# The experts' router: two parts of its weight side by side, and eight short steps instead of four

## The chip, the core and the metric

The kernel runs on one core of a Trainium2 chip. The metric is device time in microseconds (us), one launch for the whole model, median over executions. The engines are named as in the profile: PE (TensorE's matmuls), PEld (its weight loads, which can overlap matmuls), DVE (VectorE), ACT (ScalarE), POOL (GpSimd), SP (the queue that issues the DMAs).

## What is computed

Two blocks of a perceiver on 2048 tokens of 256 features, in float32. The last sub-layer is a mixture of eight experts, and the router belongs to it:

```
xt = x.reshape(2048, 256)                       # normalised rows
logits = xt @ Wr + br                           # Wr: 256 x 8
gates = entmax_bisect(logits)                   # 25 bisection steps, alpha 1.5
gates = where(gates > 1e-9, gates, 0)
h = relu(einsum('td,edf->etf', xt, W1) + b1)    # 8 experts, 256 -> 1024
y = einsum('etf,efd->etd', h, W2) + b2          # 1024 -> 256
out = einsum('etd,te->td', y, gates)
```

The gates are needed only when the experts' outputs are summed.

## The kernel before

The rows are 16 tiles (`NT`) of 128 tokens, in four chunks (`NCH`) of 512. To keep float32 accuracy on the fast matmul path each operand is kept as a high part and a low part (what rounding to fp32r left over), and a product is made of three passes, high by high, high by low, low by high (`product3`, L78 to L85). Each pass runs over two blocks `kd` of 128 features (`KD`). So a product of one tile is six matmuls.

The decoder's last stage runs on TensorE as 256 steps, 32 for each expert: `hidden(e, n)` makes 128 hidden features of one chunk (six matmuls of 128x512), and `output(e, n - 1)` multiplies the hidden features of the step before by the second weight (twelve matmuls of 128x256). The order on TensorE is written out by hand (L1158 to L1170): in step n come `hidden(n)`, `output(n - 1)`, perhaps a side step of the recurrent cell or of the transposes of the experts' input (`in_step`, L830), and perhaps a router step. Side step "ro" is the cell's output projection (L1075), "mt" turns the normalised rows of two tiles (L1063), after which ACT copies the high part (L1222) and DVE makes the low part (L1453). The side steps "ro" of chunk 3 stand in steps 16 and 17, those of "mt" of chunk 3 in steps 21 and 22.

While TensorE goes on, ACT reads each hidden block twice with ReLU, once rounded and once not (`relu`, L1246 and L1247), and POOL subtracts (`low_half`, L935) to get the low part for the third pass of `output`. DVE, after its part of the side steps, splits expert 1's weights (`split_weights`, L1473 and L1476) and then waits for the router's last result and runs the bisection (`entmax`, L1581 to L1615), with sixteen pieces of the splitting of expert 2's weights in between (`split_piece`, L1485 and L1488). Expert 2's first `hidden` waits for the last of these pieces. The gated sums (L1624) begin after that.

`router(c)` does one chunk: for each of its four tiles six matmuls, in which the tile of `xt` (128 features by 128 tokens) is loaded as the weight and eight columns of `wrs` (the router's weight, 8 columns a part) are the moving operand. All matmuls of `product3` show line L83 in the profile; the router's are those with `dec_wrs`. The results lie in `router_bank`, 8 columns for each tile. It is called in steps 17, 18, 19 and 26.

Of the kernel before, what the change touches and what calls it, by code (L numbers as in the profile page):

```python
# [12 lines left out]
F32 = mybir.dt.float32  # L13
F32R = mybir.dt.float32r
I32 = mybir.dt.int32
ALU = mybir.AluOpType
# [3 lines left out]
P = 128  # L20
D = 256
KD = D // P
# [4 lines left out]
NT = T // P  # L27
# [50 lines left out]
def product3(pe, out, lhs, rhs, first=True, last=True):  # L78

    mm = None  # L80
    for k in range(KD):
        for n, (a, b) in enumerate(PASSES):
            mm = pe.matmul(out, lhs(a, k), rhs(b, k), start=first and k == 0 and n == 0,  # L83
                           stop=last and k == KD - 1 and n == 2)
    return mm  # L85
# [624 lines left out]
def decoder(nc, k, x_sb, banks, w, out):  # L710
# [7 lines left out]
    E, F = 8, 1024  # L718
# [5 lines left out]
    with ExitStack() as ctx:  # L724
        tools = Tools(nc, ctx, "dec")
# [7 lines left out]
        xt = tools.sb("xt", [P, NCH, 2, KD, CH], F32R)  # L733
# [12 lines left out]
        gate_bias, o_bias = tools.sb("gate_bias", [P, 4]), tools.sb("o_bias", [P, 1])  # L746
        z, o, f = (tools.sb(n, [P, SEG]) for n in ("z", "o", "f"))
        b1r, b1 = tools.sb("b1r", [E * NF, P]), tools.sb("b1", [P, E * NF])
        wr, wrs = tools.sb("wr", [P, KD, E]), tools.sb("wrs", [P, 2, KD, E], F32R)
        br = tools.sb("br", [P, E])  # L750

        part = lambda n: room[:, n * KD * CH:(n + 1) * KD * CH]
# [8 lines left out]
        with ExitStack() as inner:  # L761
# [13 lines left out]
            p = att.sb("p", [P, KD, R, S2])  # L775
# [14 lines left out]
        xs, dif, sq = (moe.sb(n, [P, NT, E]) for n in ("xs", "dif", "sq"))  # L790
# [16 lines left out]
        o_psum, o_rec, o_read, w_psum, x_att = sem("o_psum"), sem("o_rec"), sem("o_read"), sem("w_psum"), sem("x_att")  # L807
        x_bo = sem("x_bo")
        late_loads, side_psum, b_cols, wr_split = sem("late_loads"), sem("side_psum"), sem("b_cols"), sem("wr_split")
# [6 lines left out]
        e_high, router_psum, gates_ready, b2_in = sem("e_high"), sem("router_psum"), sem("gates_ready"), sem("b2_in")  # L816
# [3 lines left out]
        h_bank, y_bank, router_bank = banks[2:4], banks[4:8], banks[0]  # L820
# [142 lines left out]
        def _(pe):  # L963

            def turn_rows(c):
                for i in range(4):
                    t = 4 * c + i
                    pe.wait_ge(a_xn, t + 1)
                    if t >= 4:
                        pe.wait_ge(a_xt, t - 3)  # L970
                    for kd in range(KD):
                        mm = pe.transpose(banks[4 + i][:, kd * P:(kd + 1) * P], xn_a(t)[:, kd * P:(kd + 1) * P], k.ident[:, :])
                    mm.then_inc(a_psum, 1)
# [11 lines left out]
            def keys_proj(b):  # L985
                i, half = b // 2, b % 2
                if i >= 1:
                    pe.wait_ge(c_lo, i)
                if b >= 1:
                    pe.wait_ge(v_done, b)  # L990
                for m in range(KD):
                    mm = product3(pe, proj_bank[:, m * S2:(m + 1) * S2], lambda a, kd: wk[:, a, kd, m * P:(m + 1) * P],
                                  lambda a, kd: ctx_t[:, i % 2, a, kd, half * S2:(half + 1) * S2])
                mm.then_inc(k_psum, 1)
# [113 lines left out]
                if at == NF - 1:  # L1108
                    mm.then_inc(y_psum, 1)

            def router(c):
                pe.wait_ge(wr_split, 2)
                if c == 0:
                    pe.wait_ge(x_att, NT)
                for t in range(4 * c, 4 * c + 4):
                    mm = product3(pe, router_bank[:, t * E:(t + 1) * E], lambda a, kd: xt[:, c, a, kd, t % 4 * P:(t % 4 + 1) * P],
                                  lambda a, kd: wrs[:, a, kd, :])
                mm.then_inc(router_psum, 1)

            keys_proj(0)  # L1120
            turn_rows(0)
            turn_rows(1)
# [35 lines left out]
            for n in range(1, E * STEPS):  # L1158
                e = n // STEPS
                hidden(e, n % STEPS)  # L1160
                if n == 1:
                    project_output(NT - 1)
                output((n - 1) // STEPS, (n - 1) % STEPS)
                if n - 1 in in_step:
                    if n == 1:
                        pe.wait_ge(o_read, B)
                    side_step(*in_step[n - 1])
                if n in (17, 18, 19, 26):
                    router((17, 18, 19, 26).index(n))
            output(E - 1, STEPS - 1)  # L1170

        @block.scalar
        def _(act):
# [92 lines left out]
            queries(3)  # L1266
            act.wait_ge(side_psum, 1)
            act.copy(b1[:, :], banks[7][:, 0:E * NF]).then_inc(b_cols, 1)
            act.copy(wrs[:, 0], wr[:, :, :]).then_inc(wr_split, 1)
            for b in range(B):  # L1270
                if b == 4:
                    act.wait_ge(r_const, 4)
# [19 lines left out]
            for n in range(E * STEPS):  # L1292
                e = n // STEPS
# [13 lines left out]
        def _(dve):  # L1307
# [241 lines left out]
            def late_constants():  # L1549
                dve.wait_ge(late_loads, 16 * 20)  # L1550
                dve.tensor_scalar(wp[:, :], wp[:, :], 0.5, None, ALU.mult).then_inc(r_const, 1)
                dve.tensor_scalar(o_bias[:, :], gate_bias[:, 3:4], 0.5, None, ALU.mult).then_inc(r_const, 1)
                dve.wait_ge(wr_split, 1)
                dve.tensor_tensor(wrs[:, 1], wr[:, :, :], wrs[:, 0].bitcast(F32), ALU.subtract).then_inc(wr_split, 1)

            for b in range(B):
                slot_head(b)
# [19 lines left out]
            def go(ins):  # L1577
                s.give(ins)
                dve.wait_ge(s.sem, s.n)

            def entmax():  # L1581
                dve.wait_ge(router_psum, NCH)
                go(dve.tensor_tensor(xs[:, :, :], router_bank[:, 0:NT * E].rearrange("p (t e) -> p t e", e=E),
                                     br[:, :].unsqueeze(1).to_broadcast([P, NT, E]), ALU.add))
                go(dve.tensor_scalar(xs[:, :, :], xs[:, :, :], 0.5, None, ALU.mult))
                go(dve.tensor_reduce(top[:, :], xs[:, :, :], AX.X, ALU.max))
                s.give(dve.tensor_scalar(tau[:, :], top[:, :], 1.0, None, ALU.subtract))
                go(dve.tensor_scalar(dm[:, :], top[:, :], (1.0 / E) ** 0.5, None, ALU.subtract))
                go(dve.tensor_tensor(dm[:, :], dm[:, :], tau[:, :], ALU.subtract))
                go(dve.tensor_tensor(dif[:, :, :], xs[:, :, :], each(tau), ALU.subtract))  # L1590
                go(dve.scalar_tensor_tensor(out=sq[:, :, :], in0=dif[:, :, :], scalar=0.0, in1=dif[:, :, :],
                                            op0=ALU.max, op1=ALU.mult))
                go(dve.tensor_reduce(f_lo[:, :], sq[:, :, :], AX.X, ALU.add))
                go(dve.tensor_scalar(f_lo[:, :], f_lo[:, :], 1.0, None, ALU.subtract))
                for it in range(BISECTIONS):
                    step = 0.5 ** (it + 1)
                    if 8 <= it < 24:
                        split_piece(2, it - 8)
                    go(dve.scalar_tensor_tensor(out=tau_m[:, :], in0=dm[:, :], scalar=step, in1=tau[:, :],
                                                op0=ALU.mult, op1=ALU.add))  # L1600
                    go(dve.tensor_tensor(dif[:, :, :], xs[:, :, :], each(tau_m), ALU.subtract))
                    go(dve.scalar_tensor_tensor(out=sq[:, :, :], in0=dif[:, :, :], scalar=0.0, in1=dif[:, :, :],
                                                op0=ALU.max, op1=ALU.mult))
                    go(dve.tensor_reduce(f_m[:, :], sq[:, :, :], AX.X, ALU.add))
                    go(dve.scalar_tensor_tensor(out=f_m[:, :], in0=f_m[:, :], scalar=1.0, in1=f_lo[:, :],
                                                op0=ALU.subtract, op1=ALU.mult))
                    go(dve.scalar_tensor_tensor(out=inc[:, :], in0=f_m[:, :], scalar=0.0, in1=dm[:, :],
                                                op0=ALU.is_ge, op1=ALU.mult))
                    go(dve.scalar_tensor_tensor(out=tau[:, :], in0=inc[:, :], scalar=step, in1=tau[:, :],
                                                op0=ALU.mult, op1=ALU.add))  # L1610
                go(dve.tensor_reduce(f_m[:, :], sq[:, :, :], AX.X, ALU.add))
                go(dve.reciprocal(f_m[:, :], f_m[:, :]))
                go(dve.tensor_tensor(dif[:, :, :], sq[:, :, :], each(f_m), ALU.mult))
                dve.scalar_tensor_tensor(out=xs[:, :, :], in0=dif[:, :, :], scalar=THRESH, in1=dif[:, :, :],
                                         op0=ALU.is_gt, op1=ALU.mult).then_inc(gates_ready, 1)  # L1615
# [815 lines left out]
class Shared:  # L2431
# [5 lines left out]
    def sem(self, name):  # L2437
        return self.ctx.enter_context(self.nc.semaphore(name))
# [63 lines left out]
```

## Time and profile before

| | |
|---|---|
| median of 3 runs | 2103.95 us (2100.94 to 2104.42) |
| the profiled execution's own time | 2104.26 us |
| its span, first to last instruction | 2102.5 us |
| mean granted TensorE clock | 0.986 |
| PE busy | 2043.6 us, 97% |
| PEld busy | 1833.7 us, 87% |
| DVE, ACT, POOL busy | 1206.0, 1123.9, 498.2 us |

The busy time of an engine is summed over the whole program. The granted clock is the share of full speed (2.4 GHz) that the chip gave TensorE; 0.50 is 1.2 GHz. The times of instructions further down count from the span's start.

### The profile page before, as it was taken

Reading aid. Unit: us, or ns where it says so; the run is one execution under the profiler, and the core shown is the slowest. Engines: PE = TensorE matmul, PEld = TensorE weight load, DVE = VectorE, ACT = ScalarE, POOL = GpSimd, SP = SyncE. Lnnn points to the kernel's source line nnn. Section 1 sums busy time; section 2 is a strip of 40 time slices with the busy share of each in tenths; the row PEclk is TensorE's granted clock in tenths of the full one; section 3 lists DMA queues with packets and bytes.
Section 4 is the critical chain, followed back from the end, with each engine's and each line's share of the span. In section 5 each row is a group of like instructions: output and inputs, shape, how many; then the busy total and the mean of one; then the engine's idle time right before and its main releaser. Section 6 shows DMA issues by size and latency. Waiting matters only on the chain. (4 is left out here: it accounts for less than half of the span.)

```text
span 2102.5 us, 46360 instructions
## 1 busy us (share of the span) xinstructions
PE 2043.6 (97%) x18833; PEld 1833.7 (87%) x18833; DVE 1206.0 (57%) x3625; ACT 1123.9 (53%) x2556; POOL 498.2 (24%) x411
## 2 busy tenths in 40 slices
PE   7999999999999999799899999999999999999998
PEld 7999999999999999477768888789999999999998
DVE  6756565656565654567568898734937733242311
ACT  5556555656565655333258777643544444444443
POOL 1000020000000000123311222144444444444444
PEclk9999999999999999799999999999999999999999
DMA  4000200000000000100031110100110101101000
GB/s 151 22 17 22 77 22 17 22 16 22 17 24 28 17 7 2 45 1 1 1 94 36 32 32 22 42 1 1 61 41 1 41 1 41 41 1 41 1 11 31
DMA packets 48786, 57.81 MB, mean 27 GB/s; under 512 B 6528, under 2 KB 40128, under 8 KB 48448
## 3 DMA queue, kind: packets, MB, share of 16 engines
q1 hardware_dynamic: 48576, 54.85, 8.1%
q8 instruction: 151, 2.47, 0.5%
q14 instruction: 59, 0.48, 0.1%
HBM read 46.72 MB, written 2.10 MB: 23 GB/s over the span
## 5 line engine op out<-in xcount | busy, mean ns | idle before, releaser
L935 POOL TENSOR_TENSOR right_h<-right_hr,right_h 128x512 fp32r<-128x512 f32 x256 | 341.3, 1333 | 428.5 <-ACT right_hr L1247 428.5
L1246 ACT ACTIVATE right_h<-bank,dec_b 128x512 fp32r<-128x512 f32 x256 | 176.2, 688 | 399.5 <-PE bank L83 368.5
L83 PE MATMUL bank<-lat_wv,lat_kv_t 128*128 128x256 f32 (+1 forms) x1728 | 258.9, 300 | 0.7 <-issue 0.7
L83 PE MATMUL bank<-lat_kv_t,lat_qk 128*128 128x320 f32 x1536 | 254.7, 315 | 0.0
L83 PEld LDWEIGHTS bank<-lat_kv_t,lat_qk 128*128 128x128 f32 x1536 | 226.3, 188 | 7.7
L2208 ACT ACTIVATE lat_p<-bank,lat_neg_max 128x320 f32<-128x320 f32 x256 | 136.3, 532 | 173.8 <-DVE lat_neg_max L2332 173.8
L83 PEld LDWEIGHTS bank<-lat_wv,lat_kv_t 128*128 128x128 f32 x1728 | 222.9, 190 | 6.8 <-issue 1.1
L83 PE MATMUL bank<-dec_xt,dec_lo 128*128 128x512 f32 x512 | 202.1, 395 | 0.0
L1247 ACT ACTIVATE right_hr<-bank,dec_b 128x512 f32<-128x512 f32 x256 | 174.5, 682 | 0.0
L1727 POOL TENSOR_TENSOR lat_rs_rstdc<-lat_rs_varc,lat_rs_halfc 128x4 f32<-128x4 f32 x16 | 16.2, 1015 | 635.9 <-DVE lat_rs_varc L1719 635.9
L83 PE MATMUL bank<-dec_xt,dec_hi 128*128 128x512 f32 x512 | 164.2, 402 | 0.0
L1104 PE MATMUL bank<-dec_hi,right_h 128*128 128x256 f32 x1024 | 162.6, 280 | 0.5 <-POOL right_h L935 0.5
L1104 PE MATMUL bank<-moe_hi,right_h 128*128 128x256 f32 x1024 | 161.9, 280 | 0.7 <-POOL right_h L935 0.7
L1104 PE MATMUL bank<-dec_lo,right_h 128*128 128x256 f32 x1024 | 162.4, 281 | 0.0
L83 PE MATMUL bank<-dec_xt,moe_hi 128*128 128x512 f32 x512 | 159.8, 393 | 0.0
L1104 PEld LDWEIGHTS bank<-dec_hi,right_h 128*128 128x128 f32 x1024 | 148.3, 189 | 11.2 <-POOL right_h L935 0.9
L1104 PEld LDWEIGHTS bank<-moe_hi,right_h 128*128 128x128 f32 x1024 | 147.1, 188 | 11.9 <-POOL right_h L935 0.9
L2332 DVE TENSOR_REDUCE lat_neg_max<-bank 128x1 f32<-128x320 f32 x256 | 116.9, 484 | 46.9 <-PE bank L83 46.9
L1200 ACT ACTIVATE att_p<-att_sc,att_low 128x256 f32<-128x256 f32 x256 | 113.2, 511 | 53.0 <-DVE att_low L1355 53.0
L1104 PEld LDWEIGHTS bank<-dec_lo,right_h 128*128 128x128 f32 x1024 | 138.5, 188 | 0.0
L2327 DVE TENSOR_TENSOR lat_qk<-bank,lat_qk 128x256 fp32r<-128x256 f32 x256 | 90.8, 417 | 65.6 <-ACT lat_qk L2201 65.4
L1624 DVE SCALAR_TENSOR_TENSOR x_sb<-bank,moe_xs,x_sb 128x256 f32<-128x256 f32 x96 | 41.3, 473 | 144.9 <-PE bank L1104 144.9
(322 smaller groups left out, 3920.6 us busy)
## 6 DMA issues: line engine op xcount, KB each, us to landing
raw_w<-in_L_ffn_W SPq DMA_DIRECT2D x16, 1024.0 KB, 6.5
lat_ctx_raw<-in_ctx SPq DMA_DIRECT2D x16, 512.0 KB, 4.1
right_ctx_raw<-in_ctx_turned SPq DMA_DIRECT2D x16, 512.0 KB, 3.7
lat_kv_t<-lat_lt SPq DMA_DIRECT2D x32, 128.0 KB, 2.1
out_x<-x_sb SPq DMA_DIRECT2D x4, 512.0 KB, 2.9
x_sb<-in_x SPq DMA_DIRECT2D x1, 1792.0 KB, 14.5
lat_xl_now<-lat_xl SPq DMA_DIRECT2D x7, 256.0 KB, 4.8
ahead_room<-in_L_xattn_Wq SPq DMA_DIRECT2D x1, 1024.0 KB, 7.0
```

Source lines behind the costliest of these rows:

```text
L83: mm = pe.matmul(out, lhs(a, k), rhs(b, k), start=first and k == 0 and n == 0, stop=last and k == KD - 1 and n == 2)
L935: pool.tensor_tensor(h[:, g % 2, 1, :], hr[:, g % 2, :], h[:, g % 2, 0, :].bitcast(F32), ALU.subtract).then_inc(h_lo, 1)
L1104: mm = pe.matmul(y_bank[c % 2 * 2 + i // 2][:, i % 2 * D:(i % 2 + 1) * D], h[:, n % 2, b, i * P:(i + 1) * P], w2(e % 2, a)[:, at, :], star ...
L1200: act.activation(p[:, m, r, :], sc[:, m, r, :], ACT.Exp, bias=low[:, m, r:r + 1], scale=-1.0).then_inc(p_ready, 1)
L1246: act.activation(h[:, n % 2, 0, :], h_bank[n % 2][:, :], ACT.Relu, bias=bias).then_inc(h_hi, 1)
L1247: act.activation(hr[:, n % 2, :], h_bank[n % 2][:, :], ACT.Relu, bias=bias).then_inc(h_f, 1)
L1624: dve.scalar_tensor_tensor(out=x_sb[:, t, :], in0=src(t), scalar=xs[:, t, e:e + 1], in1=x_sb[:, t, :], op0=ALU.mult, op1=ALU.add).then_inc ...
L1727: pool.tensor_tensor(self.rstd[:, :], self.vareps[:, :], self.half[:, :], ALU.pow).then_inc(self.rstd_ready, 1)
L2208: act.activation(p[:, hp % 2, h * LK:(h + 1) * LK], s_bank[h][:, 0:LK], ACT.Exp, bias=neg_max[:, u:u + 1], accum_out=rsum[:, u:u + 1]).the ...
L2327: dve.tensor_tensor(cols(1), src, cols(0).bitcast(F32), ALU.subtract).then_inc(g_lo, 1)
L2332: dve.tensor_reduce(neg_max[:, u:u + 1], s_bank[h][:, 0:LK], AX.X, ALU.max, negate=True).then_inc(s_max, 1)
```

## The change

The two parts of the router's weight lie next to each other in `wrs`: for each block `kd` the eight columns of the high part and then the eight of the low part. A tile then takes four matmuls: for each `kd` one with the tile's high part as weight and all 16 columns moving, and one with the tile's low part as weight and the eight high columns moving, which adds to the first eight result columns. A tile has 16 result columns instead of 8. `entmax` has one more operation, which adds the second eight to the first.

The work of a chunk is called in two halves of two tiles each, and the eight halves stand in steps 17, 18, 19, 20, 21, 22, 26 and 27. The semaphore `router_psum` is raised once a chunk, after its second half; `entmax` waits for all four.

```diff
-        wr, wrs = tools.sb("wr", [P, KD, E]), tools.sb("wrs", [P, 2, KD, E], F32R)
+        wr, wrs = tools.sb("wr", [P, KD, E]), tools.sb("wrs", [P, KD, 2, E], F32R)
...
-            def router(c):
-                pe.wait_ge(wr_split, 2)
-                if c == 0:
-                    pe.wait_ge(x_att, NT)
-                for t in range(4 * c, 4 * c + 4):
-                    mm = product3(pe, router_bank[:, t * E:(t + 1) * E], lambda a, kd: xt[:, c, a, kd, t % 4 * P:(t % 4 + 1) * P],
-                                  lambda a, kd: wrs[:, a, kd, :])
-                mm.then_inc(router_psum, 1)
-
+            def router(c, half):
+
+                if half == 0:
+                    pe.wait_ge(wr_split, 2)
+                    if c == 0:
+                        pe.wait_ge(x_att, NT)
+                for t in range(4 * c + 2 * half, 4 * c + 2 * half + 2):
+                    cols = slice(t % 4 * P, (t % 4 + 1) * P)
+                    for kd in range(KD):
+                        pe.matmul(router_bank[:, 2 * t * E:2 * (t + 1) * E], xt[:, c, 0, kd, cols],
+                                  wrs[:, kd].rearrange("p a e -> p (a e)"), start=kd == 0, stop=False)
+                        mm = pe.matmul(router_bank[:, 2 * t * E:(2 * t + 1) * E], xt[:, c, 1, kd, cols], wrs[:, kd, 0, :],
+                                       start=False, stop=kd == KD - 1)
+                if half == 1:
+                    mm.then_inc(router_psum, 1)
+
+            router_steps = (17, 18, 19, 20, 21, 22, 26, 27)
...
-                if n in (17, 18, 19, 26):
-                    router((17, 18, 19, 26).index(n))
+                if n in router_steps:
+                    at = router_steps.index(n)
+                    router(at // 2, at % 2)
...
-            act.copy(wrs[:, 0], wr[:, :, :]).then_inc(wr_split, 1)
+            act.copy(wrs[:, :, 0], wr[:, :, :]).then_inc(wr_split, 1)
...
-                dve.tensor_tensor(wrs[:, 1], wr[:, :, :], wrs[:, 0].bitcast(F32), ALU.subtract).then_inc(wr_split, 1)
+                dve.tensor_tensor(wrs[:, :, 1], wr[:, :, :], wrs[:, :, 0].bitcast(F32), ALU.subtract).then_inc(wr_split, 1)
...
-                go(dve.tensor_tensor(xs[:, :, :], router_bank[:, 0:NT * E].rearrange("p (t e) -> p t e", e=E),
-                                     br[:, :].unsqueeze(1).to_broadcast([P, NT, E]), ALU.add))
+                logits = router_bank[:, 0:2 * NT * E].rearrange("p (t a e) -> p t a e", a=2, e=E)
+                go(dve.tensor_tensor(xs[:, :, :], logits[:, :, 0, :], br[:, :].unsqueeze(1).to_broadcast([P, NT, E]), ALU.add))
+                go(dve.tensor_tensor(xs[:, :, :], logits[:, :, 1, :], xs[:, :, :], ALU.add))
```

## Rows read from the trace of the kernel before

**Rows 1.** The page: busy time by engine, and two lines of the 40 slices.

```profile
PE 2043.6 (97%) x18833; PEld 1833.7 (87%) x18833; DVE 1206.0 (57%) x3625; ACT 1123.9 (53%) x2556; POOL 498.2 (24%) x411
...
PEclk9999999999999999799999999999999999999999
```

**Rows 2.** Waits from 1455 us to the end: who waited for whom, us, times, longest.

```profile
PE bank L1104 <- POOL right_h L935: 0.7, 1, 0.7
```

**Rows 3.** Tile `dec_wrs`: duration in ns min/median/max, first and last start.

```profile
L83 PE MATMUL bank<-dec_wrs,dec_xt x96: 167/253/354, 1413.1 to 1455.4; 128*128 128x8 f32 x96
```

**Rows 4.** Windows: us; PE, PEld, DVE, ACT, POOL busy (x), granted clock, DMA share, GB/s.

```profile
1413.13:1415.84 2.71, 2.71 (x26) 2.71 (x25) 2.23 (x10) 0.00 (x0) 0.51 (x2) 1.00 0.00 0
1415.84:1420.27 4.43, 4.43 (x20) 3.84 (x20) 1.38 (x4) 1.27 (x2) 1.14 (x2) 0.61 0.00 0
1420.27:1422.87 2.60, 2.60 (x26) 2.60 (x25) 0.00 (x0) 0.00 (x0) 0.99 (x1) 1.00 0.00 0
1422.87:1427.32 4.45, 4.45 (x20) 3.90 (x20) 0.00 (x0) 1.26 (x2) 0.11 (x1) 0.62 0.00 0
1427.32:1430.10 2.78, 2.78 (x26) 2.78 (x25) 0.00 (x0) 0.00 (x0) 1.15 (x1) 0.93 0.00 0
1430.10:1434.33 4.23, 4.23 (x19) 3.65 (x20) 0.00 (x0) 1.22 (x2) 0.00 (x0) 0.64 0.02 4
1452.92:1455.52 2.60, 2.60 (x27) 2.60 (x25) 0.00 (x0) 0.00 (x0) 0.97 (x1) 1.00 0.02 6
1455.52:1458.34 2.82, 2.82 (x20) 2.56 (x20) 2.34 (x11) 1.10 (x2) 0.00 (x0) 1.00 0.00 0
1402.40:1405.20 2.80, 2.80 (x20) 2.54 (x19) 0.00 (x0) 1.32 (x3) 1.29 (x1) 1.00 0.00 0
```

**Rows 5.** Timeline of PE: start us, us, instructions; the first router batch and what precedes it.

```profile
1412.08 1.13 PE L1075 MATMUL bank<-dec_wp,dec_room 64*128 64x256 f32 x4
1413.13 2.84 PE L83 MATMUL bank<-dec_wrs,dec_xt 128*128 128x8 f32 x24
```

**Rows 6.** Timeline of PE: output matmuls on either side, and four transposes.

```profile
1426.38 0.63 PE L1104 MATMUL bank<-dec_lo,right_h 128*128 128x256 f32 x4
1426.85 0.63 PE L1104 MATMUL bank<-dec_hi,right_h 128*128 128x256 f32 x4
...
1437.13 0.60 PE L1063 MATMUL bank<-ident,dec_room 128*128 128x128 f32 x4
1437.49 0.71 PE L83 MATMUL bank<-dec_xt,dec_hi 128*128 128x512 f32 x2
```

**Rows 7.** Timeline of PE: steps 25 and 26, with idle before and what ended it.

```profile
1446.32 0.63 PE L83 MATMUL bank<-dec_xt,dec_hi 128*128 128x512 f32 x2
...
1449.05 0.73 PE L1104 MATMUL bank<-dec_hi,right_h 128*128 128x256 f32 x4 [0.26 <-POOL right_h L935]
1449.62 0.63 PE L83 MATMUL bank<-dec_xt,dec_hi 128*128 128x512 f32 x2
...
1452.35 0.74 PE L1104 MATMUL bank<-dec_hi,right_h 128*128 128x256 f32 x4 [0.23 <-POOL right_h L935]
```

**Rows 8.** Timeline of POOL: two of its subtractions in the same stretch.

```profile
1443.77 1.93 POOL L935 TENSOR_TENSOR right_h<-right_hr,right_h 128x512 fp32r<-128x512 f32 x1 [1.90 <-ACT right_hr L1247]
...
1449.29 3.00 POOL L935 TENSOR_TENSOR right_h<-right_hr,right_h 128x512 fp32r<-128x512 f32 x1 [0.30 <-ACT right_hr L1247]
```

**Rows 9.** Timeline of DVE: splitting of weights, first of entmax, last piece for expert 2.

```profile
1442.19 2.35 DVE L1473 CAST moe_hi<-raw_w 128x2048 fp32r<-128x2048 f32 x2
1444.46 6.68 DVE L1476 TENSOR_TENSOR dec_lo<-raw_w,moe_hi 128x2048 fp32r<-128x2048 f32 x2
1455.69 0.29 DVE L1583 TENSOR_TENSOR moe_xs<-bank,dec_br 128x128 f32<-128x128 f32 x1 [4.55 <-PE bank L83]
...
1533.06 0.69 DVE L1488 TENSOR_TENSOR dec_lo<-raw_w,dec_hi 128x512 fp32r<-128x512 f32 x1
```

**Rows 10.** Timeline of PE: expert 2's first step.

```profile
1559.09 0.63 PE L83 MATMUL bank<-dec_xt,dec_hi 128*128 128x512 f32 x2
```

## The prediction

> **What bounds the kernel now.** I read the page first: PE is busy 2043.6 of 2102.5 us, every other engine under 60% [rows 1]. A high busy share says only that something is always in the array, so the next question is whether TensorE waits in the stage that is changed. The waits from 1455 us on have one line for PE's matmuls, 0.7 us in one wait [rows 2]. So from the router to the end TensorE sets the time, and what is taken from its queue comes off the end. The third view is the tile of the router's weight, which separates its 96 matmuls from the others on L83 [rows 3]. Their durations overlap and can't be summed; their price is read from the starts of what follows them, as windows from the first matmul of a batch to the first of the next step [rows 4].
>
> Those windows show two costs. The four batches of 24 matmuls take 2.71, 2.60, 2.78 and 2.60 us. The steps of 18 matmuls behind the first three take 4.43, 4.45 and 4.23 us, where an undisturbed one takes 2.80. The reason stands in the clock column: 0.61, 0.62 and 0.64 in those three windows, 1.00 in the undisturbed one. Before each fall TensorE had a batch of matmuls with eight moving columns; it was never idle (busy 2.71 of 2.71 us). The fourth batch, alone between full steps, is followed by a step of 2.82 us at 1.00. So a batch of 2.6 us can bring the clock from 2.4 to 1.2 GHz, and does not always.
>
> **The change part by part.**
>
> *Fewer matmuls.* 96 become 64: the pass high by low joins the pass high by high. A batch at full clock takes 2.60 us for 24, or 108 ns each [rows 4]. No row shows 16 moving columns. Nearest are the 12 of `output`, four of 256 columns in 1426.85 - 1426.38 = 0.47 us, 117 ns each, and four transposes with 128 columns in 1437.49 - 1437.13 = 0.36 us, 90 ns each [rows 6]. If 32 times as many columns cost 9 ns more, 8 more should cost nothing: something other than the columns, the same for all of them, sets the pace. I take 108 ns, and keep 90 and 117 as ends. A half of 8 matmuls is then 0.87 us, and eight are 6.93 us (5.8 to 7.5). The four batches of before sum to 10.69 us. At one clock, 32 x 108 = 3.5 us are saved.
>
> *More places.* Eight switches from full matmuls to the router's and back, not four. The step behind the fourth batch shows 2.82 against 2.80 us, so 0.02 us a place. The first batch follows "ro" [rows 5] and took 0.11 us more than the second, which stays. The sum is 8 x 0.02 + 0.11 = 0.27 us (to 1.0 if each place cost the 0.11).
>
> *The clock.* Lost to it in the three steps: 4.43 + 4.45 + 4.23 - 3 x 2.80 = 4.71 us, and in the fourth step 0.02. After the change the longest run of router matmuls is 0.87 us, and a full step of 2.80 us follows each. By rows the fourth batch is nearest: 2.60 us between full steps, and the clock stayed. A third of that should stay too. One place is denser: in step 17 "ro" (1.05 us, from 1412.08 to 1413.13) and the first half stand side by side, 1.9 us together [rows 5]. "ro" alone did not bring a fall, and the 1.9 us are less than the 2.60 us at full clock. I take no falls: 4.71 us gained. The ends: all three stay (0), or one comes (3.1).
>
> So TensorE spends on routers and the disturbed steps' excess 10.69 + 4.73 = 15.42 us before, 6.93 + 0.27 = 7.20 after, a gain of 8.2 us.
>
> A rule of the Trainium skill speaks against this part. The page "TensorE: Matmul & The Clock Gate", section "Why this matters for your kernels", names idle gaps between bursts of matmuls as what lets the clock fall. By it a batch without an idle gap would not be the cause and cutting it in two would be no cure, so the sum would be the 3.5 us of fewer matmuls less the places. The trace disagrees as far as it goes: three falls, no idle time before them.
>
> *POOL's subtractions.* They take 1.93 and 3.00 us while DVE splits expert 1's weights (1442.19 to 1451.14) [rows 8, 9], and steps 25 and 26 last 3.30 us each for it (1446.32 to 1449.62, to 1452.92), 1.0 us in all [rows 4, 7]. The splitting begins after "mt" in step 22, in which a half of the router now follows: TensorE is 0.9 us later against DVE. The stretch of 9 us then covers steps 23 to 25 for the most part, and 26 less. Step 26 may lose its wait and step 24 get one. I take no change, within 0.5 us. In steps 17 to 22 each relu and subtraction had long gaps; now each step still has 2.80 + 0.87 us.
>
> *The later last result.* The last half stands in step 27, not 26, so TensorE raises it at 1458.34 - 8.2 = 1450.1 us, where it was 1455.5. DVE is free by about 1443 (its splitting moves up with "mt", some 8 us) and starts `entmax` at 1450.3, 5.4 us earlier, but 2.8 us later against TensorE. The extra addition is as large as the first of `entmax`, 0.29 us, with its semaphore 0.33 [rows 9]. The cover: expert 2's last piece begins at 1533.06 and ends by 1533.8, and expert 2 starts at 1559.09 [rows 9, 10]. 25.3 us of slack become 22.2. Without it the 3.1 us would be on the path. These edits cost nothing. The two copies into `wrs` are as large as before and move no queue; no DMA is added, and those that wait for `y_psum` move up with TensorE.
>
> **The sum.** The profiled execution: 2104.26 us, of which 1.76 lie outside its span; less 8.2, 2096.1. The median of the runs shown is 0.3 us lower, so 2095.8. The lowest run, 2100.94, is 3.3 us under the profiled one, as much as two falls: the number of falls seems to differ between executions, and the median may hold fewer than three.
>
> **The rivals.**
>
> 1. *The clock falls stay.* They come from the stretch as a whole, or from what the page's rule leaves unexplained, and three low steps remain. Gain 3.5 - 0.2 = 3.3: 2100.7 us. For it: the fourth batch of the same length had no fall, so batch length alone does not decide. Against: each fall begins at the end of a batch.
> 2. *16 columns cost twice 8.* 32 matmuls of 217 ns, so the saving in matmuls is gone: 2095.8 + 3.5 = 2099.3 us. Against: 117 ns for 256 columns.
> 3. *The wait moves to POOL.* With the routers' slack gone, steps 23 to 26 wait 0.6 us each, 2.4 instead of 1.0: 2097.2 us.
> 4. *Slower: every half brings a fall.* Six steps in a row have a half, and if a short batch is enough for a fall, up to eight steps run at 1.2 GHz. At 1.57 us each that is 12.6 us in place of 4.7, less 3.5: 2104.0 + 4.6 = 2108.6 us. It decides from the sixth fall on (8.2 / 1.57 = 5.2). Against: a batch of 2.60 us that left the clock alone.
> 5. *One fall stays*, at step 17 after "ro": 2097.4 us.
>
> **How the numbers follow.** No falls, 108 ns: 0.62. One fall or POOL: 0.16. Dearer columns: 0.06. Two or three falls, or a median of before that held fewer: 0.12. Every half falls: 0.04. The range reaches from 2093.3 (90 ns each, and the waits for POOL gone) to 2100.0, which leaves out rival 4 and most of rival 1. About 0.2% (4.2 us) is what a measurement here can tell from no change: rival 1 and a part of the dearer cases lie within it, 0.14; slower 0.04; faster 0.82.
>
> **What the profile of the changed kernel would show.** 64 router matmuls, each half some 0.87 us from its first start to the next step's first; steps 18 to 23 about 2.8 us behind it at a clock of 1.00; mean clock nearer 0.99 than 0.986 if nothing else moves; `entmax` starting near 1450 us, expert 2 near 1551. Halves of over 1 us would mean dearer columns; a step of 4.4 us, a fall. PE waiting for `right_h` more than 1.0 us in steps 23 to 27 would be rival 3. A wait of TensorE for DVE at expert 2 would show the cover mis-sized.

## The result, and the profile after

The changed kernel took 2092.8 us, median of 6 executions (2092.52 to 2096.95), against 2102.92 us for the kernel before (6 executions, 2100.94 to 2109.54). The ratio is 0.9947, 95% interval 0.9933 to 0.996: faster by 0.53%, some 11 us; the two medians are 10.1 us apart. I had forecast 2095.8 and a range from 2093.3 to 2100.0, so the direction was right and the time lies 0.5 us under the range.

The page of the changed kernel, to be read against [rows 1]:

```profile
PE 2030.2 (97%) x18801; PEld 1822.3 (87%) x18801; DVE 1206.1 (58%) x3626; ACT 1123.8 (54%) x2556; POOL 498.0 (24%) x411
...
PEclk9999999999999999899999999999999999999999
```

There are 32 matmuls fewer. PE is busy 13.4 us less, more than 32 matmuls can be.

The windows of PE in the changed kernel, to be read against [rows 4]. The columns are start and end, length, PE busy (x), granted clock, DMA share, GB/s. First the stage from 838 to 1060 us, then the 50 us from the side step "ro" of step 17 on, two halves of the router each with the step behind it, and last steps 24 and 25:

```profile
838.00:1060.00 222.00, 195.21 (x1095) 0.94 0.05 14
1408.32:1458.32 50.00, 48.77 (x330) 1.00 0.00 1
...
1409.38:1410.30 0.92, 0.92 (x10) 1.00 0.00 0
1410.30:1413.14 2.84, 2.84 (x21) 1.00 0.00 0
1413.14:1413.95 0.81, 0.81 (x11) 1.00 0.00 0
1413.95:1416.79 2.84, 2.84 (x20) 1.00 0.00 0
1432.39:1436.41 4.02, 3.04 (x20) 1.00 0.00 0
1436.41:1439.72 3.31, 3.06 (x21) 1.00 0.00 0
```

The clock is 1.00 throughout the router's stretch. The first half takes 0.92 us, the next 0.81. Steps 24 and 25, which hold no router work, take 4.02 and 3.31 us: the wait for POOL has moved and grown. The timelines of PE, POOL and DVE show it, and the start of expert 2:

```profile
1408.32 1.13 PE L1075 MATMUL bank<-dec_wp,dec_room 64*128 64x256 f32 x4
...
1435.84 0.73 PE L1104 MATMUL bank<-dec_hi,right_h 128*128 128x256 f32 x4 [0.97 <-POOL right_h L935]
...
1439.14 0.74 PE L1104 MATMUL bank<-dec_hi,right_h 128*128 128x256 f32 x4 [0.25 <-POOL right_h L935]
...
1432.59 6.50 POOL L935 TENSOR_TENSOR right_h<-right_hr,right_h 128x512 fp32r<-128x512 f32 x2 [2.88 <-ACT right_hr L1256]
...
1432.38 5.56 DVE L1485 TENSOR_TENSOR dec_lo<-raw_w,moe_hi 128x2048 fp32r<-128x2048 f32 x2
1447.19 0.29 DVE L1593 TENSOR_TENSOR moe_xs<-bank,dec_br 128x128 f32<-128x128 f32 x1 [9.25 <-PE bank L1122]
1447.51 0.29 DVE L1594 TENSOR_TENSOR moe_xs<-bank,moe_xs 128x128 f32<-128x128 f32 x1
...
1547.80 0.63 PE L83 MATMUL bank<-dec_xt,dec_hi 128*128 128x512 f32 x2
```

**Where the 11.3 us of the two profiled spans lie.** Take two marks that both kernels have: "ro" of step 17 and the first matmul of expert 2. Before they stand at 1412.08 and 1559.09 us [rows 5, 10], after at 1408.32 and 1547.80. From mark to mark it is 147.01 us before and 139.48 after, 7.53 less. The other 3.76 us are there before the first mark. Up to there the change touches none of TensorE's instructions, only the two that fill `wrs`. When the first of them runs, 3.2 of the 3.76 us are already there (tile `dec_wr`, before and then after):

```profile
L1269 ACT CAST dec_wrs<-dec_wr x1: 208/208/208, 1079.8 to 1079.8; 128x16 fp32r<-128x16 f32 x1
```

```profile
L1278 ACT CAST dec_wrs<-dec_wr x1: 207/207/207, 1076.6 to 1076.6; 128x16 fp32r<-128x16 f32 x1
```

The experiments had to say what those 3.76 us are, and how much of the 7.53 is clock.

### The profile page after: what moved, and what is told of

The parts are those of the page before. It is cut to its first block and busy times, and to the rows that moved or that the text cites. A ratio compares the mean times of both kernels' runs of the same rounds, so it can differ in the third digit from the quotient of the medians.

```text
span 2091.2 us, 46297 instructions
## 1 busy us (share of the span) xinstructions
PE 2030.2 (97%) x18801; PEld 1822.3 (87%) x18801; DVE 1206.1 (58%) x3626; ACT 1123.8 (54%) x2556; POOL 498.0 (24%) x411
```

## The experiments

Below, "the stretch" is the time from the last "ro" to expert 2, and "low time" is worked out from a window's granted clock c and length w as 2(1 - c)w, the time that TensorE spent at 1.2 GHz; half of it is time lost. Clocks have two digits, so low time is known to about 1 us in a window of 50 us.

### The kernels against themselves

`aa_before` is the kernel before, run as if it were new; `before_third` is one more profile of it; `again_after` is the changed kernel once more. No edit.

> The kernel before, unchanged, run as if it were another. Theory (the router's stretch explains the whole gain and the executions differ only by how many clock falls they hold): ratio 1.000 within 0.2%, the times spread over some 3 us or more, and the second profile shows another number of low stretches than the first, in the stage from 838 to 1060 us (the linear-attention and feed-forward stage) too, though no instruction differs. Rival (the program decides the falls in that stage): the same low stretches at the same places as in the first profile.

> The kernel before, one more look. Theory: the router is reached at 1408.3 to 1413.8 us, the later the more low clock lies between 838 and 1060 us; three or four falls in the router's stretch; 146 to 147.5 us from the first router matmul to expert 2. Rival: fewer falls, which would make the gain of the change smaller than the two profiles show.

> The changed kernel once more. Theory: 0.995 to 0.996 against before on the same chip, with no clock fall from step 17 to 28, and low stretches between 838 and 1060 us that differ in number from those of its first profile. If the 3.75 us by which its first profile reached the router earlier belong to chance, this profile reaches the router at another time than 1409.4 us. Rival: it reaches it at 1409.4 us again, since something in the program has changed that stage.

`aa_before`: 2104.35 us (12 executions, 2100.96 to 2108.63), ratio 1.0001, interval 0.999 to 1.0011. `again_after`: 2096.01 us (6 executions, 2092.09 to 2097.19), ratio 0.9954, interval 0.994 to 0.9968. `before_third`: one time, 2105.57 us.

The windows of PE, same columns: the stage from 838 to 1060 us and the 50 us from the last "ro" on. First the profiled execution of before:

```profile
838.00:1060.00 222.00, 197.19 (x1081) 0.91 0.04 12
1412.08:1462.08 50.00, 49.51 (x312) 0.90 0.00 1
```

`aa_before`, the same program:

```profile
838.00:1060.00 222.00, 194.33 (x1095) 0.95 0.05 15
1407.38:1457.38 50.00, 49.49 (x302) 0.86 0.00 1
```

`before_third`, the same again:

```profile
838.00:1060.00 222.00, 195.07 (x1096) 0.94 0.06 14
1408.64:1458.64 50.00, 49.53 (x285) 0.80 0.00 1
```

`again_after`:

```profile
838.00:1060.00 222.00, 193.93 (x1091) 0.93 0.04 14
1409.79:1459.79 50.00, 48.77 (x330) 1.00 0.00 1
```

Low time in the router's 50 us is 10, 14 and 20 us in three executions of one program, and 0 in both of the changed kernel. The stretches are 147.01, 148.60 and 151.75 us against 139.48 and 139.43. Counted from the first router matmul, as in the expectation, `before_third` takes 150.70 us, where I had expected 146 to 147.5. In `before_third` even the fourth batch, which left the clock alone in the first profile, is slowed itself and followed by a slow step:

```profile
1451.04 3.54 PE L83 MATMUL bank<-dec_wrs,dec_xt 128*128 128x8 f32 x24
...
1455.86 1.05 PE L83 MATMUL bank<-dec_xt,dec_hi 128*128 128x512 f32 x2
```

The other column answers the 3.76 us. The clock from 838 to 1060 us is 0.91, 0.95 and 0.94 in three executions of the kernel before, and 0.94 and 0.93 in two of the changed one. Over all fourteen profiles, in which TensorE has the same instructions up to there, the mark "ro" comes the later the lower that clock is: 1412.08 and 1412.69 at 0.91; 1409.79 and 1410.12 at 0.93; 1408.21 to 1409.23 at 0.94 (five profiles); 1407.29 to 1407.84 at 0.95 (five). The 3.76 us are the difference between one execution and another, not an effect of the change. Nothing differs behind the second mark: in all fourteen profiles the execution's own time is the start of expert 2 plus 545.14 to 545.19 us. So an execution's time has two parts that vary, the mark and the stretch.

### Each half of the change alone

`side_only` has the 16 columns, but whole chunks in steps 17, 18, 19 and 26 (`side_again`: one more profile). `eight_only` has the eight steps, but `product3` with 96 matmuls.

```diff
 side_only, against the changed kernel
-            router_steps = (17, 18, 19, 20, 21, 22, 26, 27)
+            router_steps = (17, 18, 19, 26)
...
-                    router(at // 2, at % 2)
+                    router(router_steps.index(n), 0)
+                    router(router_steps.index(n), 1)
```

```diff
 eight_only, against the kernel before
-            def router(c):
+            def router(c, half):
...
-                for t in range(4 * c, 4 * c + 4):
+                for t in range(4 * c + 2 * half, 4 * c + 2 * half + 2):
...
+            router_steps = (17, 18, 19, 20, 21, 22, 26, 27)
...
-                if n in (17, 18, 19, 26):
-                    router((17, 18, 19, 26).index(n))
+                if n in router_steps:
+                    at = router_steps.index(n)
+                    router(at // 2, at % 2)
```

> Only the first half of the change: both parts side by side as 16 columns, four matmuls a tile, but still whole chunks of four tiles in steps 17, 18, 19 and 26. A batch is 16 matmuls, some 1.8 us. Theory (a shorter batch does not lower the clock, whatever makes it shorter): all of the fast-clock gain already comes with this half, no step behind a batch at a clock under 0.9, and the ratio is that of the whole change, near 0.995 to 0.996. Rival (the spreading over eight steps is what keeps the clock up): falls behind the batches stay, gain 3.5 us or 0.17% (0.998).

> The first half of the change alone (steps 17, 18, 19, 26) once more, one look. Theory (falls depend on how the batches lie in time, which differs between executions): another number or other places of falls than the two of its first profile if the stage before ends at another time. Rival: again one behind step 17 and one behind step 26.

> Only the second half of the change: the six matmuls a tile of before, two tiles in each of eight steps. A batch is 12 matmuls, some 1.3 us; the number of matmuls stays 96. Theory: no falls behind the batches, the 3.5 us of fewer matmuls are missing, so a gain of 4 to 5 us where three falls go (0.9975 to 0.998). Rival (the number of matmuls is what counts): ratio 1.000, falls still there.

`side_only`: 2095.39 us (6 executions, 2094.34 to 2099.91), ratio 0.9958, interval 0.9942 to 0.9973. `side_again`: 2094.82 us, once. `eight_only`: 2096.99 us (6 executions, 2096.6 to 2097.47), ratio 0.9962, interval 0.9949 to 0.9974. The windows of PE in `side_only`, then in `eight_only`, where two windows with the busy times of all engines follow: the batch of step 17, and what comes behind it:

```profile
1407.29:1457.29 50.00, 49.53 (x314) 0.93 0.00 1
```

```profile
1407.77:1457.77 50.00, 49.21 (x330) 0.97 0.00 1
...
1408.83:1410.25 1.42, 1.42 (x14) 1.42 (x13) 1.28 (x3) 0.00 (x0) 0.36 (x1) 1.00 0.00 0
1410.25:1414.50 4.25, 4.25 (x18) 3.72 (x18) 2.34 (x12) 1.27 (x2) 1.31 (x2) 0.60 0.00 0
```

The stretches are 141.90 and 141.84 us for the 16 columns, 144.13 for the eight steps, 139.48 and 139.43 for both parts. My expectation that the shorter batch of `side_only` leaves no fall was wrong: 7 us of low time remain, behind the batch of step 17 and behind that of step 26, in both profiles. In `eight_only`, where I had expected none, 3 us remain, behind the one batch that follows "ro" (1408.83 to 1410.19 us by its starts, at full clock). So the two parts of the change overlap. Against the mean stretch of before, 149.12 us, the 16 columns save 7.2 us, of which some 3.5 are matmuls; the eight steps save 5.0; both together save 9.7, and at these places only both together left no low time. The ratios (0.9958, 0.9962, and 0.9947 and 0.9954 for both) have intervals that overlap and don't rank them. For `eight_only` I had expected 0.9975 to 0.998: I had counted only the three falls of the first profile. `side_again`'s places of falls are those of the first profile, as its rival had it; it also reached "ro" at nearly the same time, 1407.84 against 1407.29, so it does not tell the two views apart.

### Where a batch stands, and how long it is

`apart`: the kernel before with its four batches in steps 18, 21, 24 and 27. `eight_later`: `eight_only` in steps 18 to 23, 26 and 27. `one_batch`: the changed kernel's 64 matmuls all in step 27.

```diff
 apart
-                if n in (17, 18, 19, 26):
-                    router((17, 18, 19, 26).index(n))
+                if n in (18, 21, 24, 27):
+                    router((18, 21, 24, 27).index(n))
```

```diff
 eight_later, against eight_only
-            router_steps = (17, 18, 19, 20, 21, 22, 26, 27)
+            router_steps = (18, 19, 20, 21, 22, 23, 26, 27)
```

```diff
 one_batch, against the changed kernel
-                if n in router_steps:
-                    at = router_steps.index(n)
-                    router(at // 2, at % 2)
+                if n == 27:
+                    for at in range(8):
+                        router(at // 2, at % 2)
```

> The kernel before with its four batches of 24 matmuls set apart: steps 18, 21, 24 and 27 instead of 17, 18, 19 and 26, so that no side step ro stands before the first and two full steps lie between each pair. Theory (a batch of 2.6 us can bring a fall by itself, when and whether depending on how it happens to lie in time): still one to three falls, ratio 0.998 to 1.000. Rival (falls come from low stretches that lie close together): none, ratio 0.997.

> Eight steps of twelve matmuls with product3, as in the run with the second half of the change alone, but in steps 18 to 23, 26 and 27, so that none stands behind the side step ro of step 17. That run had one fall, at the end of the batch behind ro. Theory (ro and the batch behind it count together): no fall, some 1.6 us less from the first router step on, ratio 0.9955 against 0.9962. Rival (any batch of 1.3 us can do it): a fall in one of the steps 18 to 23, same ratio.

> The changed kernel's 64 matmuls all in one batch of some 7.1 us in step 27. Theory (the length of a batch decides): one or two falls in the batch and behind it, 2 to 4 us more than the changed kernel from there to expert 2, and nothing of the clock's gain kept beyond what four falls cost before: ratio 0.996 to 0.9975. Rival (falls are a matter of the stretch, not of the batch): none, and a ratio as the changed kernel's.

`apart`: 2098.8 us (11 executions), ratio 0.9974, interval 0.9964 to 0.9984. `eight_later`: 2095.56 us (5), ratio 0.9962, interval 0.995 to 0.9975. `one_batch`: 2099.26 us (11), ratio 0.9984, interval 0.9975 to 0.9992.

The timeline of PE in `apart`, three of the four batches, each with the matmuls behind it:

```profile
1414.03 3.10 PE L83 MATMUL bank<-dec_wrs,dec_xt 128*128 128x8 f32 x24
1416.99 1.20 PE L83 MATMUL bank<-dec_xt,dec_hi 128*128 128x512 f32 x2
...
1428.56 2.82 PE L83 MATMUL bank<-dec_wrs,dec_xt 128*128 128x8 f32 x24
1431.24 0.71 PE L83 MATMUL bank<-dec_xt,dec_hi 128*128 128x512 f32 x2
...
1440.12 2.73 PE L83 MATMUL bank<-dec_wrs,dec_xt 128*128 128x8 f32 x24
1442.71 0.71 PE L83 MATMUL bank<-dec_xt,dec_hi 128*128 128x512 f32 x2
...
1443.49 0.99 PE L83 MATMUL bank<-dec_xt,dec_hi 128*128 128x512 f32 x2
```

With full steps on both sides, the first batch brings the clock down at once, the second not at all, the third after a delay (0.99 us for a pair that takes 0.62 at full clock), and the fourth, not shown, not. So a fall needs no second batch nearby, and batches of the same 24 matmuls brought it at two places of four. The stretch is 145.97 us, 1.04 less than in the first profile of before, at the same 10 us of low time. The two waits for POOL are gone, which were worth 1.0 us. The ratio is better than the 0.998 to 1.000 that I had expected. The windows of the three kernels give 0.90, 1.00 and 0.86: `apart`, `eight_later`, `one_batch`.

```profile
1410.12:1460.12 50.00, 50.00 (x319) 0.90 0.00 1
```

```profile
1409.23:1459.23 50.00, 50.00 (x349) 1.00 0.00 1
```

```profile
1408.21:1458.21 50.00, 49.49 (x293) 0.86 0.00 1
```

`eight_later` agrees with the reading of step 17: away from "ro" none of its eight batches of 12 matmuls brings a fall. This is one profile, and those of before differ among themselves. The stretch is 141.18 us, not 144.13. That is more than the 1.6 us of one fall, since two waits for POOL (0.56 and 0.23 us in `eight_only`'s timeline) are gone as well: a batch now stands in step 23. Its ratio is not better than `eight_only`'s, 0.9962 both; the median is 1.4 us lower, less than the intervals can tell. `one_batch` has all 64 matmuls of the change and keeps 1.6 thousandths of its five: with 14 us of low time the stretch is 145.18 us, 5.7 more than the changed kernel's. Here the number of matmuls is that of the change; only their place differs. I had expected 2 to 4 us more and a ratio of 0.996 to 0.9975, so the one batch costs more than I thought.

### Filling the waits for POOL

`fill`: the changed kernel with its halves in steps 17 to 24, and a wait on `m_lo` ahead of the last chunk's first half. `fill_later`: the same in steps 18 to 25. `side_later`: `side_only` in steps 18, 20, 22 and 24.

```diff
 fill, against the changed kernel
+                    if c == NCH - 1:
+                        pe.wait_ge(m_lo, 2 * NCH)
...
-            router_steps = (17, 18, 19, 20, 21, 22, 26, 27)
+            router_steps = (17, 18, 19, 20, 21, 22, 23, 24)
```

> The changed kernel with the last chunk's two halves in steps 23 and 24 instead of 26 and 27 (one more wait, on m_lo, which hidden would do in step 24 anyway). In the changed kernel TensorE waits for POOL's slow subtractions in steps 24 and 25, some 1.2 and 0.5 us. Theory (a half laid in front of such a wait is paid for by the wait): 1 to 1.6 us less than the changed kernel between the first router matmul and expert 2 (137.0 us against 138.4), ratio 0.9945 to 0.995. Rival (POOL slows by as much, since the subtractions then overlap more of DVE's splitting): no difference, 138.4 us.

> Eight halves in steps 18 to 25. Theory: as steps 17 to 24, 137.0 us from the first router matmul of step 17's place to expert 2 within 0.3, since no execution of the halves showed a fall even behind ro and the waits for POOL are covered in both; ratio 0.995. Rival (the half behind ro costs a fall in some executions): faster than steps 17 to 24 by up to 1.6 us in those.

> Both parts side by side, whole chunks (16 matmuls, 1.8 us), in steps 18, 20, 22 and 24: none behind the side step ro, each with a full step on either side, two of them ahead of TensorE's waits for POOL. Theory (1.8 us are still long enough for a fall in some executions; in a profile of the half-change at steps 17, 18, 19 and 26 two of the four batches brought one): times spread more than the version with eight halves, and none to two falls in the profile; ratio about 0.9955. Rival (only a batch next to other thin work falls): no fall, and as fast as eight halves laid in front of the waits, 0.995.

`fill`: 2091.93 us (5 executions, 2090.15 to 2096.52), ratio 0.995, interval 0.9937 to 0.9964. `fill_later`: 2091.46 us (5), ratio 0.9947, interval 0.9931 to 0.9963. `side_later`: 2091.19 us (5, 2090.31 to 2093.31), ratio 0.9943, interval 0.993 to 0.9956.

The timeline of POOL in `fill`:

```profile
1436.95 3.23 POOL L935 TENSOR_TENSOR right_h<-right_hr,right_h 128x512 fp32r<-128x512 f32 x1 [2.88 <-ACT right_hr L1258]
1440.63 2.85 POOL L935 TENSOR_TENSOR right_h<-right_hr,right_h 128x512 fp32r<-128x512 f32 x1 [0.45 <-ACT right_hr L1258]
```

And of PE in `fill`, the second and third four of step 24's twelve output matmuls; the third needs POOL's result:

```profile
1439.50 0.63 PE L1104 MATMUL bank<-dec_lo,right_h 128*128 128x256 f32 x4
1440.24 0.73 PE L1104 MATMUL bank<-dec_hi,right_h 128*128 128x256 f32 x4
```

The subtractions are as slow as in the changed kernel, and the half in front of each now pays for most of it. Some 0.4 us stay: the third four start 0.74 us after the second, where 0.47 is usual, just behind the end of POOL's subtraction (1440.18). Step 24 takes 3.24 us in `fill` and `fill_later` and 3.15 in `side_later`, where a full step takes 2.80 to 2.90. The stretches are 138.11, 138.11 and 138.02 us, against 139.48 and 139.43 of the changed kernel. `fill` is what its theory said, 137.0 us from the first router matmul of step 17 on. `fill_later` is no shorter, so in the profile of `fill` the half behind "ro" costs nothing. These three are the shortest that I measured, and `side_later`, with four batches of 16 matmuls, is as short as the two with eight halves: away from "ro" and from the waits, its profile had no fall, and its times spread less than those of the halves, where I had expected more. By the executions' times their lead over the changed kernel (0.9 to 4.8 us between medians) is inside the intervals of the ratios, so it rests on the profiled stretches.

## Why the prediction was wrong, point by point

The changed kernel was forecast by its mechanisms rightly, and mis-sized in what it was compared with.

**The step that failed is the one on the clock**, "Lost to it in the three steps: 4.43 + 4.45 + 4.23 - 3 x 2.80 = 4.71 us". It took one execution's falls for the kernel's. In three profiles of the kernel before, the low time of 10, 14 and 20 us means some 5, 7 and 10 us lost. The stretch is 147.01, 148.60 and 151.75 us, while the changed kernel's is 139.48 and 139.43. The local gain is therefore 7.5, 9.1 or 12.3 us, by which execution of before is taken. The mean, 149.12 - 139.46 = 9.7 us where 8.2 were forecast, fits the two ratios, which make it 9.7 and 11.1 us. The shape of the range followed: it reached 4.2 us up for missing gain and 2.5 down, and the downward part held cheaper matmuls and the waits for POOL gone, and no further falls of before.

**The same mistake stands in the sum**, "The profiled execution: 2104.26 us, ... less 8.2, 2096.1". In total that execution was typical of before, 0.3 us over the median of the runs shown, but it was made of a late mark (1412.08 us, where the fourteen profiles have 1409.0 in the mean) and the shortest of three stretches. The change shortens only the stretch. The changed kernel's profiled execution, 2092.97 us, lies 3.1 us under the 2096.1: its mark came 3.76 us earlier, and its stretch is 0.67 us longer than the forecast had it. So chance in the stage before had its part in putting the median under the range. I had also read the lowest run, 2100.94 us, as one with fewer falls, and feared that the median may hold fewer than three. `aa_before` shows the contrary: its profiled execution took 2101.15 us and holds more low time in the router's stretch than the first, 14 us against 10. It was short by its mark, 1407.38.

**The second set of six** came out at 2096.01 us, next to the 2095.8 forecast; the twelve executions of both sets together have a median of 2094.65. The changed kernel has no falls in its router in either profile and still spreads from 2092.09 to 2097.19. The profiles put such a spread before the mark: `fill` and `fill_later` have the same stretch, 138.11 us, their marks are 4.96 us apart (1412.69 and 1407.73), and so are their times (2095.95 and 2090.99). The mark goes with the clock of the stage from 838 to 1060 us, which is 0.91 to 0.95 from one profile to another.

**The fourth batch** was my nearest row for a batch that leaves the clock alone. `before_third` shows it bringing a fall. The conclusion that I drew, that a batch a third as long is safe, held in both profiles of the changed kernel, even behind "ro", but not by that row. For the batches of 12 and 16 matmuls the place made a difference. Twelve brought a fall behind "ro" (`eight_only`) and at no other place. Sixteen brought one behind "ro" and one in step 26, behind a step with a wait (`side_only`), and none at the four places of `side_later`.

**Matmuls: right.** Expected 6.93 us for the halves and 0.27 for their places, 7.20; measured 6.77 for the eight halves (0.92, 0.89 and 0.90 behind side steps, 0.81 or 0.82 elsewhere) and 0.45 for the slightly longer steps behind them, 7.22. 16 moving columns cost what 8 do, which rules rival 2 out. Without falls on either side, 96 matmuls in `eight_later` against 64 in `fill`, both in eight places, the batches sum to 10.24 and 6.75 us, 3.5 apart as forecast. The stretches differ by 3.07, for `fill` keeps some 0.4 us of wait in step 24.

**POOL: partly rival 3.** I put the term at no change, within 0.5 us; it measured 0.73 more. Steps 24 and 25 now take 4.02 and 3.31 us, 1.73 over two undisturbed ones, where 1.0 was lost before. I had counted only that DVE's splitting would cover less of the later steps, not that the subtraction of step 23 would start just with DVE's slow part (1432.59 against 1432.38). The rest of the balance closes: 15.42 - 7.22 - 0.73 = 7.47 us against 7.53 measured.

**Rivals 1, 4 and 5.** No half brought a fall in the changed kernel's two profiles. Rival 5 was seen in `eight_only` at its very place, step 17, and in `side_only` there too. The page "TensorE: Matmul & The Clock Gate" of the Trainium skill, section "Why this matters for your kernels", names idle gaps as the thing to avoid; by that rule no placement of busy matmuls should matter. The runs disagree: TensorE was busy 1.42 of 1.42 us before the fall in `eight_only`, and 64 equal matmuls cost 5.7 us more in one batch than in eight. That the place decides in single batches rests on one or two profiles of each placement, and is likely, not shown.

**DVE and the later last result: right in effect.** `entmax` starts at 1447.19 us after waiting 9.25 us for the router, the added operation takes 0.29 us and starts 0.32 after the first, and TensorE waits for none of it at expert 2.

## What to carry to other kernels

Matmuls with few moving columns can cost twice: their own time, and now and then a stretch at half clock behind them. Lay them in short groups between full matmuls, away from other thin work, and best in front of a wait that is there anyway. A clock fall seen in one profile has no fixed price: profile the same program two or three times and price the spread, for the kernel before as much as for the one after. And compare two profiles between marks around the change, so that what happened before the first mark isn't credited to it.

## What the runs showed of the hardware

- One program's low time in the same 50 us was 10, 14 and 20 us in three executions. Of four batches of 24 matmuls between full steps in `apart`, two brought a fall and two did not. What decides it wasn't settled here.
- In fourteen profiles the mark "ro" moved by 5.4 us with the clock of the stage from 838 to 1060 us (0.91 to 0.95), for the same instructions of TensorE.
- 8 and 16 moving columns with a 128x128 float32 weight take the same: 8 matmuls, half of them with 16 columns, take 0.81 us, and 24 with 8 columns take 2.60, 101 and 108 ns each.
- POOL's 128x512 subtraction takes 1.27 us alone and 3.23 us in `fill` beside DVE's 128x2048 subtraction.
